# Values of two units taken as a pair on TensorE, and an opening with four blocks turned by VectorE

## The reference

```python
xn = layernorm(x)                                   # over the last axis
q, k, v = xn @ wq, xn @ wk, xn @ wv                 # 16, 4 and 4 heads of 16
q, k = rope(q), rope(k)                             # pairs (8 + 8) turned by position
k, v = repeated over 4 groups to 16 heads
attn = softmax(causal(q k^T / sqrt(16)))
out = x + (attn v) @ wo + real(ifft(fft(xn) @ w)) + bias
```

## Time and profile before

| what | value |
|---|---|
| median of 3 runs | 1010.68 us (1005.64 to 1014.27) |
| the profiled execution | 1008.69 us |
| its span, from the first to the last instruction | 1006.9 us |
| busy in the span | PE 961.0, DVE 737.4, ACT 650.7, POOL 325.1 us |
| granted TensorE clock, mean | 0.956 of full speed |
| first values of a unit on TensorE | 69.83 us from the span's start |

### The profile page before, as it was taken

One profiled execution on the slowest core, in us unless ns is written; L12 is line 12 of the kernel. 1 busy time (PEld: TensorE's weight loads), 2 busy tenths in 40 slices (PEclk: granted clock), 3 DMA queues, 4 the chain that ended last, 5 costly groups with the idle time before them and its releaser, 6 DMA issues.

```text
span 1006.9 us, 17764 instructions
## 1 busy us (share of the span) xinstructions
PE 961.0 (95%) x6792; PEld 471.1 (47%) x6792; DVE 737.4 (73%) x894; ACT 650.7 (65%) x1303; POOL 325.1 (32%) x350
## 2 busy tenths in 40 slices
PE   8989899999999989999999999999999999999998
PEld 6644455445444434443354554544444444544424
DVE  7686677767787787777888776677878887788801
ACT  2433566664676655676777666676767766677785
POOL 6287683868136300133500132327210100100000
PEclk9867699999999996999999999999999997999989
DMA  5645005152211210010200311001510000000000
GB/s 162 138 136 107 23 32 106 44 109 70 67 35 48 58 13 17 12 48 2 68 17 6 64 44 49 12 11 34 95 34 11 2 1 1 12 12 1 1 1 22
DMA packets 37701, 43.50 MB, mean 43 GB/s; under 512 B 11376, under 2 KB 23280, under 8 KB 37616
## 3 DMA queue, kind: packets, MB, share of 16 engines
q1 hardware_dynamic: 37616, 42.36, 17.2%
HBM read 27.13 MB, written 14.68 MB: 42 GB/s over the span
## 4 chain that ended last, share of the span: by engine, by line
PE 84%; ACT 8%; DVE 5%; issue 2%; DMA 0%; SPq 0%; POOL 0%; ACTq 0%
PE psO L1357 28%; PE psA L1293 20%; PE psS L1340 18%; ACT prob_sb L975 6%; PE psS L1266 4%; PE psS L1325 3%; PE psS L1327 2%; DVE pmax L1102 2%; PE psA L1298 2%; DVE pmax L1104 2%; PE psS L1273 1%; PE psA L1308 1%; ACT oraw_sb L984 1%; PE psS L1317 1%; PE psA L1365 1%
## 5 line engine op out<-in xcount | busy, mean ns | idle before, releaser
L975 ACT ACTIVATE prob_sb<-psS 128x512 f32<-128x512 f32 (+2 forms) x1108 | 560.0, 586 | 226.3 <-PE psS L1340 223.6
L1104 DVE TENSOR_REDUCE pmax<-psA 128x2 f32<-128x1024 f32 x384 | 459.9, 1220 | 116.9 <-PE psA L1293 115.7
L1340 PE MATMUL psS<-q_st,k_st 50*128 50x512 f32 (+3 forms) x1232 | 397.9, 432 | 5.2 <-ACT prob_sb L975 4.3
L1293 PE MATMUL psA<-k_st,q_st 48*128 48x512 f32 (+3 forms) x1280 | 360.7, 428 | 15.6 <-DVE pmax L1104 7.0
L1357 PE MATMUL psO<-prob_sb,v_sb 128*17 128x512 f32 (+3 forms) x2560 | 305.8, 551 | 15.5 <-ACT prob_sb L975 7.7
L1293 PEld LDWEIGHTS psA<-k_st,q_st 48*128 48x128 f32 x1280 | 177.9, 193 | 249.1 <-DVE pmax L1104 90.0
L1102 DVE TENSOR_REDUCE pmax<-psA 128x4 f32<-128x512 f32 (+2 forms) x192 | 198.7, 1046 | 87.0 <-PE psA L1298 85.9
L859 POOL TENSOR_SCALAR_AFFINE_SELECT prob_sb<-prob_sb 128x512 f32<-128x512 f32 x128 | 81.1, 635 | 499.2 <-ACT prob_sb L975 487.2
L1340 PEld LDWEIGHTS psS<-q_st,k_st 50*128 50x128 f32 x1232 | 195.0, 192 | 93.7 <-ACT prob_sb L975 83.4
L1357 PEld LDWEIGHTS psO<-prob_sb,v_sb 128*17 128x17 f32 x2560 | 43.2, 96 | 104.4 <-issue 40.9
L1298 PE MATMUL psA<-mask_r,mask_l 64*128 64x64 bf16 (+1 forms) x768 | 80.3, 213 | 0.0
(11 more groups left out here) (106 smaller groups left out, 570.3 us busy)
## 6 DMA issues: line engine op xcount, KB each, us to landing
q_st<-parts_scratch SPq DMA_DIRECT2D x174, 64.0 KB, 2.5
parts_scratch<-parts SPq DMA_DIRECT2D x64, 128.0 KB
k_st<-parts_scratch SPq DMA_DIRECT2D x48, 128.0 KB, 4.4
q_st<-spartT SPq DMA_DIRECT2D x256, 2.0 KB
x_sb<-in_L_attn_x SPq DMA_DIRECT2D x7, 512.0 KB, 4.1
out<-x_sb SPq DMA_DIRECT2D x14, 256.0 KB, 2.3
parts_scratch<-parts SPq DMA_DIRECT2D x32, 64.0 KB
oraw_sb<-in_L_attn_x SPq DMA_DIRECT2D x1, 1536.0 KB, 11.7
```

The costliest lines, as they stand in the source:

```text
L975: nc.scalar.activation(prob[:, g % DEEP, r0:r0 + hp, s0:CH], bank_at(bank)[:, 0:hp * w].rearrange("p (h s) -> p h s", h=hp), ACT.Exp).then ...
L1104: nc.vector.reduce_max(pmax[:, heads[0]:heads[0] + 3:2, i, q], psA[:, two:two + 2, :], AX.X).then_inc(S["a_free"], 1)
L1293: last = mm(bank[:, k * w:(k + 1) * w], q_st[lo:lo + ROWS, n % (2 * KV), heads[o * per + k] % 2, i * P:(i + 1) * P], k_st[lo:lo + ROWS, sl ...
L1340: last = mm(bank[:, h * w:(h + 1) * w], k_st[lo:lo + FULL, key_slot(n, tile), kv, tile % CT * P:(tile % CT + 1) * P], q_st[lo:lo + FULL, n ...
```

## The change

It does two things.

First, in the order of the work: v_ready() lets the values of an even unit be due only when the exponentials (and the mask) of the next unit are due as well, and the values of the odd unit are taken straight behind them when they are ready. The functions values(), scores() and exps() themselves, with their waits, stay as they are.

Second, in the opening: VectorE turns block 3 as well (FIRST), and GpSimd begins with block 4. Projection 4 moves into the opening, and the lists of all engines there are put in another order. The statistics of chunks 2 to 5 are sampled behind the four turns; those of chunks 6 and 7, and all that follows from chunks 2 to 7, stand behind the shift of step 0 (before: chunks 2 and 3 in the opening, chunks 4 to 7 behind the shift of step 1). The two large loads of x for them are issued ahead of the first stores. The key rows of slots 0 and 1 are filled by ScalarE, and the sign of the sine table is set by GpSimd where it repeats the table, so that ScalarE copies each sine block at once. Warm-up matmuls are 10 and 20 in two places instead of 44.

```diff
-    STATS_AT = 1
...
-    WARM = 44
+    WARM = (10, 20)
...
-    OPENING = [("rope", 0, 0), ("rope", 1, 0), ("t", 0, 0), ("t", 0, 1), ("qk", 0), ("qk", 1), ("qk", 2)]
-    OPENING += [("rope", m, k) for m in range(2) for k in range(1, NJ)]
-    OPENING += [("v", 0), ("t", 1, 0), ("t", 1, 1), ("qk", 3)]
+    OPENING = [("rope", 0, 0), ("rope", 1, 0), ("t", 0, 0), ("t", 0, 1), ("qk", 0), ("qk", 1), ("rope", 0, 1), ("rope", 1, 1)]
+    OPENING += [("t", 1, 0), ("t", 1, 1), ("qk", 2)]
+    OPENING += [("rope", 0, 2), ("rope", 1, 2), ("rope", 0, 3), ("rope", 1, 3), ("qk", 3), ("qk", 4), ("v", 0)]
...
-        stage = [("qk", 4), ("v", 1), ("qk", 5)]
+        stage = [("qk", 5), ("v", 1)]
...
             if UNITS[n][u][3] is not None:
                 at = mask_at.get(g, big)
+            if g % 2 == 0:
+                at = max(at, (exp_at if UNITS[n][u + 1][3] is None else mask_at).get(g + 1, big))
...
             elif aside and pe and pe[-1][0] == "pv" and now - aside_at > 2.5 and act - now > 0.5:
                 choice = aside
+            elif ready["v"] <= soon and next_v % 2 == 1 and pe[-1] == ("pv", next_v - 1):
+                choice = "v"
             elif ready["a"] <= soon and dve - now < 1.4:
...
-        FIRST = (0, 1, 2)
+        FIRST = (0, 1, 2, 3)
...
             sp.dma_start(wo_sb[:, :, :], wo.rearrange("(c p) n -> p c n", p=P)).then_inc(S["wo_in"], 16)
+            sp.dma_start(x_two, x_v[:, BTILES:BTILES + TWO, :]).then_inc(S["x_two_in"], 16)
+            sp.dma_start(x_last, x_v[:, BTILES + TWO:2 * BTILES, :]).then_inc(S["x_two_in"], 16)
             store(0)
             store(1)
             load_k(0)
             store(2)
-            for rest in (False, True):
+            load_first_q(0, False)
+            load_first_q(1, False)
+            store(3)
+            for rest in (True,):
                 for t in range(2):
                     load_first_q(t, rest)
-            sp.dma_start(x_two, x_v[:, BTILES:BTILES + TWO, :]).then_inc(S["x_two_in"], 16)
-            sp.dma_start(x_last, x_v[:, BTILES + TWO:2 * BTILES, :]).then_inc(S["x_two_in"], 16)
...
+            pool.wait_ge(S["first_parts"], 2 * len(FIRST))
+            before, masks, adds, biases = ("start",), 0, 0, 0
...
             for m in range(2):
                 for c in range(KC):
                     copy_first(m, c)
-            copy_v(0)
-            copy_xnT(1, 0)
-            copy_xnT(1, 1)
+                copy_qk(3 + m)
+                ones_rows(1, m)
...
             for job in ACT_ORDER:
                 if job == ROOTS_JOB:
-                    roots(BTILES, CHUNKS * CT, 3)
+                    roots(2 * CT, CHUNKS * CT, 2)
...
-            newton(0, CT, 0)
-            dve.wait_ge(S["newton"], 5)
-            normalise(0)
             for c in range(KC):
...
+            newton(0, CT, 0)
+            dve.wait_ge(S["newton"], 5)
+            normalise(0)
+            sample(CT, 2 * CT)
+            moments(CT, 2 * CT)
...
-            rotate(2)
-            moments(2 * CT, BTILES, 2)
-            newton(2 * CT, BTILES, 2)
+            for m in FIRST:
+                rotate(m)
+            sample(2 * CT, 6 * CT)
             for v in range(len(SEQ_A)):
+                if v == LAST_USE[0] + 1:
+                    sample(6 * CT, CHUNKS * CT)
+                    moments(2 * CT, CHUNKS * CT)
                 if v == ROOTS_BACK:
-                    newton(BTILES, CHUNKS * CT, 3)
+                    newton(2 * CT, CHUNKS * CT, 2)
```

More of the change, by code:

```diff
@@ L477, in schedule @@
                 first = min(ready.values())
-                assert first < big, (ready, next_b, next_v, next_a, stage[:1], back[:1])
+                if first >= big:
+                    now += 0.5
+                    assert now < 5000.0, (ready, next_b, next_v, next_a, stage[:1], back[:1])
+                    continue
                 choice = min(("a", "b", "v"), key=lambda k: ready[k])
@@ L877, in _ @@
             pool.wait_ge(S["rest_in"], 32)
[L878 to L886, removed]
+            pool.wait_ge(S["xn_first"], CT)
+            repeat = rope_sb[:, :, CT:BTILES, :].rearrange("p m t (o n) -> p m t o n", o=1)
+            nc.gpsimd.tensor_copy(rep_cos, repeat[:, 0].broadcast_to([P, BTILES - CT, P // N8, N8])).then_inc(S["rest_ready"], 1)
+            for to, span in ((rep_sin, slice(0, 2 * CT)), (rep_sin_rest, slice(2 * CT, 3 * CT))):
+                source = repeat[:, 1, span].broadcast_to([P, span.stop - span.start, P // N8 // 2, N8])
+                nc.gpsimd.tensor_copy(to[:, :, 0:N8, :], source).then_inc(S["rest_ready"], 1)
+                nc.gpsimd.tensor_scalar(to[:, :, N8:2 * N8, :], source, -1.0, None, ALU.mult).then_inc(S["rest_ready"], 1)
+            pool.wait_ge(S["rest_ready"], 5)
+            pool.wait_ge(S["first_parts"], 2 * len(FIRST))
+            before, masks, adds, biases = ("start",), 0, 0, 0
             for job in POOL_ORDER:
-                if job[0] == "ones" or (job[0] == "r" and job[2] in (1, 2)):
+                if before[0] != "start" and (job[0] == "ones" or (job[0] == "r" and job[2] in (1, 2))):
                     pool.wait_ge(*done_by(before, masks, adds, biases))
@@ L917, in tables @@
                     bank = bank.rearrange("p (t s) -> p t s", t=CT)
[L918 to L922, removed]
+                    nc.scalar.activation(rest, bank, ACT.Copy).then_inc(S["bank_free"], 1)
             def copy_xnT(cc, c):
@@ L989, in copy_first, with ones_rows @@
                                      scale=(1.0 if m == 0 else -1.0) / D).then_inc(S["t_copied"], 1)
+            def ones_rows(slot, t):
+                half = slice(t * HALF + 32, (t + 1) * HALF)
+                nc.scalar.activation(k_st[half, slot, :, :].rearrange("p g s -> p (g s)"), ident[half, 0:1].broadcast_to([32, KV * CH]), ACT.Copy,
+                                     scale=0.0, bias=-1.0).then_inc(S["ones_first"], 1)
+            act.wait_ge(S["ident_ready"], 2)
+            ones_rows(0, 0)
+            ones_rows(0, 1)
             roots(0, CT, 0)
@@ L995, in _ @@
             copy_xnT(0, 1)
+            roots(CT, 2 * CT, 1)
             copy_qk(0)
             copy_qk(1)
-            roots(CT, 2 * CT, 1)
+            tables(0, 1)
+            tables(1, 1)
+            copy_xnT(1, 0)
+            copy_xnT(1, 1)
             copy_qk(2)
-            for m in range(2):
-                for k in range(1, NJ):
-                    tables(m, k)
+            for k in range(2, NJ):
+                tables(0, k)
+                tables(1, k)
             for m in range(2):
@@ L1160, in _ @@
             spread(1)
-            moments(0, CT, 0)
+            sample(0, CT)
+            moments(0, CT)
             dve.wait_ge(S["wqk_in"], 32)
@@ L1398, in _, with warm @@
             pe.wait_ge(S["ident_ready"], 2)
-            for _ in range(WARM):
-                mm(psA[:, 3, 0:P], ident[:, :], ident[:, :], start=True, stop=True)
+            def warm(count):
+                for _ in range(count):
+                    mm(psA[:, 3, 0:P], ident[:, :], ident[:, :], start=True, stop=True)
+            warm(WARM[0])
             pe.wait_ge(S["rep_ready"], 4)
```

84 lines of the change are left out of this document (44 added, 40 removed).

## The result

The changed kernel takes 1048.62 us (median of 4 runs, 1045.19 to 1056.08), the kernel before 1009.62 in the same series. The ratio is 1.0379 (95% interval 1.0325 to 1.0433): 3.8% slower. The forecast was 982, faster.

A forecast was written before the change was run, and what follows sets the result against it. The prediction took ScalarE's loop over three score banks to bound a step. Its terms, +35-57-8+1 = -29 us on the profiled 1008.69, gave 979.7, forecast as 982 for the median; range 952 to 1016.

The forecast's parts named there:

- A step is bound by a loop: Attention steps: ScalarE empties three score banks, TensorE refills none while values run; a gap of 0.62 us a unit.
- Rival 3: Attention steps: starved score banks decide, 0.5 us more gap a pair (+80), a third hidden (-41); 1042 us, chance 0.16.
- The switch: TensorE between scores and values: 0.3 us there and back, about 158 switches go, 47 us less TensorE work.
- The gap of a pair: ScalarE's gap while paired values run: 1.48 us instead of 1.24 for two singles; +35 us over 160 pairs.
- VectorE mostly stays fed: During paired values: two maxima slots hold at most 2.4 us of work against some 1.8 us of values.
- Other work hidden, -57 us: Outputs and projections in TensorE's freed time: a little under half of 124 us hidden; bounds 0 and -110.
- rival 2: Pairs cost the loop what they give elsewhere, or hardly form; only the opening is left: 1003 us, chance 0.24.
- the last unit: End of the kernel: the last pair waits for the last unit's exponentials, +1 us, bounds 0 and +2.
- The opening, -8 us: Start of the kernel: shifts -5.8, projection 4 -3.4, later start of TensorE's list +1.2; bounds -18 and +10.
- the statistics behind step 0's shift: Opening, VectorE: second-half statistics partly in idle time, the rest covered by step 0's exponentials: 0; uncovered some 5 us.
- The 5.8 us of late shifts: Opening, SyncE's queue: chunk 1 loads come at least 7 us earlier, so shifts of steps 2 and 3 go unhindered: -5.8.
- The feared 12 us behind the 2 MB: Opening: 2 MB of x issued ahead of the first stores hold the one queue for 12 us; behind the +10 bound.

The follow-up runs named there:

- experiment 3: ScalarE's exponentials, VectorE's maxima or both halved, in the kernel before and with pairs (old opening): pairs minus singles +45.7, +28.0, -13.4 us; whole work +41.9.
- the order kept: Kernel before with its planned order, only the values of every even unit moved down ahead of the odd one's: 1079.51 us, ratio 1.07.
- narrow pairs alone: Kernel before with its planned order, values moved into pairs only where two units have 768 columns or less together: 1023.16 us, ratio 1.0142.

## Why the prediction was wrong

- **What bounds the kernel.** "A step is bound by a loop: ScalarE empties three score banks" was half of it. I took two steps of equal length, one with VectorE busy for 34.1 us and one with 24.7, as proof that VectorE plays no part. It proved only that ScalarE's loop is enough by itself. VectorE's slots are a second loop of nearly the same length: by experiment 3 it alone keeps the whole cost of the pairs, and ScalarE's alone two thirds. Rival 3 named the mechanism that won, starved buffers, but of ScalarE alone, and gave 1042. I had given it 0.16. Its 1042 is near 1048.62 in part by luck: it has +80 us of gaps and 41 hidden, where the runs show less of both (below).
- **The switch.** Half shown. A wide pair takes 1.84 us where two single values take 2 x 0.98, as forecast. The 47 us for about 158 switches (149 in the list that the planner made) were seen nowhere: with slack on both consumers the pairs gain 13 us, and in the last two steps without other work they gain nothing.
- **The gap of a pair.** Nearly right where the clock was full: 1.23 to 1.48 us measured, 1.48 forecast; a step without other work 42.7, 42 forecast. By my scale of 20 such steps, (42.7-40.4) x 20 = +46 us, +35 forecast. With the step of 45.2 at a clock of 0.92 counted in, the three are 3.2 us longer than before in the mean, which makes +63; so the term is +46 to +63 with what the clock adds.
- **"VectorE mostly stays fed".** Wrong. Its waits grew from 201.6 to 255.1 us. Two slots hold 2.4 us only if both have just been filled when the pair begins. The planner puts scores for the maxima ahead of values only while VectorE has less than 1.4 us of work by its model (`dve - now < 1.4`), and a wide pair takes 1.84.
- **Other work hidden, -57 us.** This is the step that failed most. The step with a chunk's output from 868.5 is still 10.9 us longer than its neighbour, where it was 12.3: a tenth hidden and not a half. The forecast named this sign ("still 12 us longer") and gave it to rival 2. One pair of steps is a weak measure, though: the other such step (394.7 to 447.8) takes 53.1 us, and in the kernel with pairs alone the two take 53.1 and 50.5, beside steps without other work of 42.8 to 46.9. What they share is that none came down to the 48 forecast. The sum tells more: with the same opening the pairs cost 1048.62-1009.51 = 39 us, of which the last unit is 1; gaps of +46 to +63 then leave 8 to 25 us hidden, and not 57 (an estimate from these runs; no run measures it by itself). The likely reason, argued and not measured, is that a free stretch is of use only if the other engines have work meanwhile, and here both had just been starved and needed scores first.
- **A term that was missing: the clock.** I let the clock only rise. In the stretch from 140 us it was low for 71 us more (98 against 27). A wide pair then takes 3.18 us and not 1.84, and nothing is fed meanwhile. Summed from the start of each group of values to the next instruction, values took 265.8 us in that stretch after and 252.0 before, although 135 groups of two should have saved about 16 (0.12 each): some 30 us of the loss is there. 19 of the 153 groups began at the lower level, 4 of 286 before. It overlaps with the gaps, so the terms don't add up to 41.5 exactly.
- **The opening, -8 us.** It was -1 (0.997, interval 0.9932 to 1.0008). The term that I had put at 0 failed first: the statistics behind step 0's shift. I looked at whether the exponentials cover VectorE's work, and not at who waits for its result. TensorE waited 4.89 us for VectorE ahead of the maxima of step 1 (61.69), and GpSimd 8.31 us for the statistics with the masks of step 0 behind it, so that the first values came at 80.86 and not near 66. The 5.8 us of late shifts did not come back but grew to 11, because the order of SyncE's list, and not the turned blocks alone, set when the loads of chunk 1 went out: behind the shift of step 1. In the forecast I had moved the loads by the time that GpSimd saved, without reading what stands ahead of them in the queue. Most of these losses were made up by step 4. The feared 12 us behind the 2 MB did not appear: the first stores were issued at 23.25 and the loads of keys at 30.00, where they were at 24.54 and 31.29.
- **The range.** 952 to 1016 does not follow from the bounds named with it. A tenth hidden and 0.4 us more gap a pair give 64-12-8+1 = +45 us, some 1055, which holds the measured 1048.62; three quarters and no gap give some 910.
- **The Trainium skill's rule** (TensorEngine Tiling (Array Packing), PSUM Bottleneck), which says that a faster TensorE can leave the emptying of PSUM as the bottleneck, was weighed and given too little. The runs agree with it: the same pairs cost 42 us with the emptying as it is, and gain 13 us with half of it on both engines.

## What to carry to other kernels

An engine that feeds two others through small rings can't be read by the length of its own work: here, joining two of its phases saved a switch and starved both rings for the longer phase. To find out who binds, relieve each consumer alone and then both; a step that keeps its length when one engine has less to do shows that another loop suffices, not that the first is harmless. Before time is called free for other work, look at whether the consumers are full at that moment; before a DMA is called early, read what stands ahead of it in its queue; and before work is moved back on one engine, read which other engine's list waits for its result.

## What I had not expected of the hardware

The granted clock fell with the pairs, though TensorE had the same arithmetic in fewer phases: the profiled executions show means of 0.956 before, 0.956 with the opening alone, 0.932 changed, 0.935 with pairs alone, 0.915 with the order kept, and back to 0.969 for the pairs with both consumers relieved. It fell after stretches in which TensorE had waited for banks: ahead of the pair at 964.82, which ran at the lower level, a score matmul at 960.10 is followed by the next only 0.58 us later, and ahead of a like one at 868.47 the one at 864.61 by 0.97. This is what stood ahead of two falls and no rule: most gaps of that length in this trace are followed by none. Nor is the lower clock all of the cost: the kernel with narrow pairs alone is 10.8 us longer from step 4's first values to the last step's, with 24 us at the lower level where there were 27. For the wide pairs, whether the clock is a cause or only follows the waits was not separated; a kernel that keeps TensorE busy during the waits was not run.
